# Grouped attention in a two-layer decoder: head turns moved between the two sides of the probability turns

## The chip, the cores and the metric

The kernel runs on one core of one Trainium2 chip. The metric is the device time of one execution in microseconds; the median of three runs before the change is 1094.67 us (1092.79 to 1095.51). The engines are TensorE (PE, with its weight load PEld), VectorE (DVE), ScalarE (ACT), GpSimd (POOL) and SyncE (SP), which issues most of the DMAs. Each engine works through its own list of instructions in order; semaphores tie the lists together.

## The reference

A decoder of two layers over four sequences of 256 tokens of width 256: a recurrent gate, experts chosen by token, a ternary projection, causal attention with 16 heads, grouped attention, a mixture of experts. The change touches only the grouped attention, which is, for 8 groups g of 2 query heads each and head width 128:

```python
q = _ln(_fp8_linear_pertensor(ln_out, wq, ...), qln_w, qln_b)    # (b, s, g, 2, 128)
k = _ln(_fp8_linear_pertensor(ln_out, wk, ...), kln_w, kln_b)    # (b, s, g, 128)
v = _fp8_linear_pertensor(ln_out, wv, ...)
core = _gqa(q, k, v)             # softmax(q k / sqrt(128)) v, per head
qx = _ln(_fp8_linear_pertensor(ln_out, wqx, ...), qxln_w, qxln_b)
kx, vx = split(einsum('bsi,oi->bso', ctx, w_kv_x)); kx = _ln(kx, kxln_w, kxln_b)
xout = _gqa(qx, kx, vx)
cat = concatenate([core, xout])
return einsum('bsi,oi->bso', _div_clamp_fp8(cat, proj_smooth), wproj) * (...)
```

"Side 0" is the attention over the tokens themselves (q, k, v), "side 1" the one over the context (qx, kx, vx). In each of them the head vectors are divided by their own root of the variance; the mean is taken out by centring the weights.

## The kernel before

The function front_stage holds everything but the mixture of experts. Its last part is a pipeline over 32 items, one for each group and sequence (four sequences of group 0, then four of group 1, and so on). A Slot n works on three items at once: it projects item n, scores item n-1, averages item n-2 and adds the output of item n-3. Slots 0 to 31 project, slots 1 to 32 score, slots 2 to 33 average, slots 3 to 34 output. There are 35 slots. In slots 0 to 27 the weights of the next group are also turned (transposed) and split into a high and a low half, two fills a slot: weights 0 and 1 in the first slot of a group, 2 and 3 in the second, 4 and 5 in the third, 6 and 7 in the fourth. I call these slots 0/1, 2/3, 4/5 and 6/7. Slot n with n mod 4 = 1 is a slot 2/3.

The order of each engine is written out by hand in its own function visit:

- PE (line 877): the first half of the projection (project_item(o, 0), L799 and L814), the two weight fills (next_weights, L765 and L767), the turns of the probabilities of item n-2 (turn_item_probs, L825: side 0 in two fills, then side 1 in two fills, four turns of 128x128 each), the second half of the projection, the turns of the heads of item n-1 (turn_item_heads, L838: three fills of four turns), in slot 1 alone two fills of tokens (L555), then average_item (L849), output_item (L873) and score_item (L861).
- ACT (line 1139): the high halves of the weights (L1066, L1074; weights 4 and 5 are only copied, L1070), the first copy of each side of the turned probabilities (take_item_probs, L1094), squares with their sums and the values from the projection's four fills (take_projection, L1086 and L1088), queries and keys from the head fills (take_item_heads, L1101, L1108, L1101), the averages (L1122), the exponentials of both sides (softmax_item, L1134).
- DVE (line 1496): the low halves of the weights (take_weight, L1437 and L1442; called w_lo in this text; none for weights 4 and 5), the second copy of each side of the probabilities (L1454), the rounding of the averages to fp8 (quantise_item, L1469, L196 to L199), the normalisation of the heads, read from all four projection fills (normalise_item, L1462), the addition of the output (add_item, L1494), the maxima of the scores (item_max, L1476), the division by the softmax sums, called the finish (finish_softmax, L1483 and L1486, once for each side). In slot 1 the fp8 rounding of the second half of the tokens (quantise, L1420 to L1425) follows the normalisation.
- POOL: one root per item (head_scale, L1662 and L1663), after the last squares, before the normalisation; and the split of the rounded tokens (L1669).

All results of PE go to PSUM, eight banks of 128x512 floats. The class Fills holds the plan: a fill has a bank and a number, and PE may start it (claim) when the fill before it in that bank has been drained by its reader. plan_slot (line 280) sets the order. The projection uses banks 0 to 3. All else turns round in banks 4 to 7, by the helper ring, which gives fill j of a slot bank 4 + j mod 4:

```python
WEIGHTS, PROBS_T, HEADS_T, OUT, ADD, SCORES = 0, 2, 6, 9, 11, 12
```

So the weights lie in banks 4 and 5, the probabilities of side 0 in 6 and 7, those of side 1 in 4 and 5, the heads in 6, 7 and 4, the averages in 5 and 6, the output in 7, the scores in 4 to 7. turn_item_heads also waits until the normalisation of the item before has drained the four projection fills; score_item waits until queries and keys are read; average_item waits until both copies of a side are made.

Of the kernel before, what the change touches and what calls it, by code (L numbers as in the profile page):

```python
# [28 lines left out]
ACT = mybir.ActivationFunctionType  # L29
# [250 lines left out]
def plan_slot(f, o):  # L280


    def ring(*fills_of):
        for j in fills_of:
            f.plan(4 + j % 4, ("slot", o.n, j))

    if o.projects:
        f.plan(0, ("proj", o.n, 0))
        f.plan(1, ("proj", o.n, 1))
    if o.n == 0:  # L290
        f.plan(4, ("Yc", 1, 0))
        f.plan(5, ("Yc", 1, 1))
    if o.weights:
        ring(WEIGHTS, WEIGHTS + 1)
    if o.averages:
        ring(*range(PROBS_T, HEADS_T))
    if o.projects:
        f.plan(2, ("proj", o.n, 2))
        f.plan(3, ("proj", o.n, 3))
    if o.scores:  # L300
        ring(*range(HEADS_T, OUT))
    if o.n == 1:
        f.plan(5, ("xT", "Q", 1, 0))
        f.plan(6, ("xT", "Q", 1, 1))
    if o.averages:
        ring(OUT, OUT + 1)
    if o.outputs:
        ring(ADD)
    if o.scores:
        ring(*range(SCORES, SCORES + 4))  # L310
# [93 lines left out]
def front_stage(nc, c, a):  # L404

    with Stage(nc) as st:
# [88 lines left out]
        with nc.Block() as block:  # L495
# [52 lines left out]
            def _(pe):  # L548
# [268 lines left out]

                def turn_item_probs(o):
                    for side in range(2):
                        pe.wait_ge(probs_ready, 2 * o.n + (side - 3))  # L820
                        for kt in range(2):
                            name = ("slot", o.n, PROBS_T + 2 * side + kt)
                            bank = fills.claim(pe, name)
                            for i in range(4):
                                last = pe.transpose(c.ps[:, bank, i * P:(i + 1) * P],  # L825
                                                    c.probs[:, side, i // 2, i % 2, kt * P:(kt + 1) * P], c.ident[:])
                            fills.filled(last, name)

# [48 lines left out]
                def visit(o):  # L877
# [6 lines left out]
                    if o.averages:  # L884
                        turn_item_probs(o)
                    if o.projects:
                        project_item(o, 1)
                    if o.scores:
                        turn_item_heads(o)
                    if o.n == 1:  # L890
# [60 lines left out]
            def _(act):  # L951
# [137 lines left out]

                def take_item_probs(o):  # L1090
                    for i in (0, 2):
                        name = ("slot", o.n, PROBS_T + i)
                        bank = fills.wait_full(act, name)
                        fills.drain(act.activation(c.probsT[:, i, :], c.ps[:, bank, :], ACT.Copy), name)  # L1094

# [43 lines left out]
                def visit(o):  # L1139
# [7 lines left out]
                    if o.averages:  # L1147
                        take_item_probs(o)
                    if o.projects:
                        take_projection(o, 0)  # L1150
                        take_projection(o, 1)
                    if o.scores:
                        take_item_heads(o)
                    if o.n == 1:
# [71 lines left out]
            def _(v):  # L1226
# [222 lines left out]

                def take_item_probs(o):  # L1450
                    for i in (1, 3):
                        name = ("slot", o.n, PROBS_T + i)
                        bank = fills.wait_full(v, name)
                        fills.drain(v.tensor_copy(c.probsT[:, i, :], c.ps[:, bank, :]), name)  # L1454

# [40 lines left out]
                def visit(o):  # L1496
                    if o.weights:
                        next_weights(o)
                    if o.averages:
                        take_item_probs(o)  # L1500
                    if o.outputs:
                        quantise_item(o)
                    if o.projects:
                        normalise_item(o)
# [533 lines left out]
```

## Time and profile before

| | before |
|---|---|
| median of three runs | 1094.67 us |
| the profiled execution's own time | 1086.79 us |
| its span, first to last instruction | 1085.2 us |
| PE busy | 968.6 us, 89% |
| DVE busy | 702.7 us, 65% |
| ACT busy | 596.6 us, 55% |
| POOL busy | 127.8 us, 12% |

Busy time counts what an engine executes, not what it waits for. PE's instructions overlap in its pipeline: the end of one lies behind the start of the next, so a row's length of n instructions is the sum of their intervals and a tail. The idle time in square brackets is that just before the row's first instruction, with the instruction whose semaphore ended it. The grouped part reaches from about 307 us (slot 0) to 960 us.

### The profile page before, as it was taken

How to read it: one execution, taken by the hardware profiler on the slowest of the kernel's cores; microseconds unless marked ns; L12 is line 12 of the kernel's file. 1: busy time of each engine (PE TensorE's matmuls, PEld its weight loads, DVE VectorE, ACT ScalarE, POOL GpSimd, SP SyncE). 2: the span in 40 equal slices, each digit the busy share in tenths (PEclk: the TensorE clock that was granted, in tenths of full speed). 3: DMA queues.
4: the chain of work that ended last, by engine and by line, in shares of the span. 5: the costliest groups of instructions: out<-in, count | busy, mean ns of one | idle time of the engine just before them, and what ended most of it. 6: DMA issues, size and time to landing. Idle time of an engine off the chain costs nothing. (4 is left out here: it accounts for less than half of the span.)

```text
span 1085.2 us, 16461 instructions
## 1 busy us (share of the span) xinstructions
PE 968.6 (89%) x5766; PEld 738.8 (68%) x5766; DVE 702.7 (65%) x1575; ACT 596.6 (55%) x2166; POOL 127.8 (12%) x126
## 2 busy tenths in 40 slices
PE   6989987998756899999999999999999999759597
PEld 3656655575545788878788888878888787544354
DVE  4655535577865676767676776767777676646554
ACT  4342324454625676767767676776767676413131
POOL 2000201000132211010101001010111101000000
PEclk9999997999887799999999999999999999869899
DMA  6010000000100010100100100100100300000000
GB/s 200 1 59 1 0 1 1 2 2 2 60 1 1 1 60 1 50 11 1 60 1 1 60 1 1 60 1 2 59 1 2 110 7 1 1 1 0 20 0 19
DMA packets 23122, 23.23 MB, mean 21 GB/s; under 512 B 3010, under 2 KB 22019, under 8 KB 23043
## 3 DMA queue, kind: packets, MB, share of 16 engines
q1 hardware_dynamic: 22944, 22.17, 6.5%
q8 instruction: 46, 0.75, 0.3%
q14 instruction: 34, 0.27, 0.1%
q10 hardware_dynamic: 98, 0.03, 0.0%
HBM read 21.15 MB, written 1.05 MB: 20 GB/s over the span
## 5 line engine op out<-in xcount | busy, mean ns | idle before, releaser
L1134 ACT ACTIVATE group_probs<-ps,score_bias 128x256 f32<-128x256 f32 x256 | 117.3, 484 | 112.5 <-DVE score_bias L1476 112.5
L799 PE MATMUL ps<-group_w_hi,xq 128*128 128x256 f32 (+1 forms) x512 | 133.4, 301 | 18.7 <-POOL xq L1669 11.2
L799 PE MATMUL ps<-group_w_lo,xq 128*128 128x256 f32 (+1 forms) x512 | 123.9, 284 | 0.0
L1462 DVE TENSOR_TENSOR group_heads<-ps,head_rstd 128x384 f32<-128x384 f32 x128 | 62.4, 550 | 87.0 <-POOL head_rstd L1663 87.0
L849 PE MATMUL ps<-group_probsT,group_values 128*128 128x512 f32 x256 | 116.7, 599 | 0.8 <-issue 0.8
L861 PE MATMUL ps<-group_kT,group_qT 128*128 128x256 f32 x512 | 115.9, 379 | 1.1 <-ACT group_qT L1101 1.1
L799 PEld LDWEIGHTS ps<-group_w_hi,xq 128*128 128x128 f32 x512 | 100.3, 196 | 21.2 <-DVE group_heads L1462 7.9
L1086 ACT ACTIVATE group_squares<-ps 128x128 f32<-128x128 f32 x384 | 106.5, 321 | 13.3 <-PE ps L799 11.9
L861 PEld LDWEIGHTS ps<-group_kT,group_qT 128*128 128x128 f32 x512 | 95.0, 190 | 13.5 <-issue 1.8
L1476 DVE TENSOR_REDUCE score_bias<-ps 128x2 f32<-128x512 f32 x128 | 88.2, 691 | 21.1 <-PE ps L861 21.1
L799 PEld LDWEIGHTS ps<-group_w_lo,xq 128*128 128x128 f32 x512 | 100.6, 196 | 0.7
L1086 ACT ACTIVATION_READ_ACCUMULATOR group_squares<-ps 128x1 f32 x384 | 93.3, 254 | 0.0
L825 PE MATMUL ps<-ident,group_probs 128*128 128x128 f32 x512 | 71.7, 281 | 18.2 <-DVE group_probs L1486 8.7
L873 PE MATMUL ps<-group_wp_hi,group_cat 128*128 128x256 f32 x256 | 76.4, 335 | 4.0 <-DVE group_cat L199 4.0
L849 PEld LDWEIGHTS ps<-group_probsT,group_values 128*128 128x128 f32 x256 | 46.8, 193 | 47.9 <-issue 47.9
L825 PEld LDWEIGHTS ps<-ident,group_probs 128*128 128x128 f32 x512 | 57.4, 143 | 29.3 <-DVE group_probs L1486 22.7
L1486 DVE TENSOR_SCALAR group_probs<-group_probs,score_inv 128x256 f32<-128x256 f32 x256 | 73.1, 349 | 2.3
L1663 POOL TENSOR_TENSOR head_rstd<-head_sum,minus_half 128x12 f32<-128x12 f32 x32 | 72.7, 2271 | 2.7
L1122 ACT ACTIVATE group_cat_y<-ps,vec_inv 128x256 bf16<-128x256 f32 x128 | 57.1, 528 | 24.9 <-PE ps L849 23.7
L814 PE MATMUL ps<-group_w_x,ctxT 128*128 128x256 f32 x256 | 67.3, 386 | 0.0
L1662 POOL TENSOR_SCALAR head_sum<-head_sum 128x12 f32<-128x12 f32 x32 | 6.5, 202 | 493.0 <-ACT group_values L1088 493.0
L873 PE MATMUL ps<-group_wp_lo,group_cat 128*128 128x256 f32 x256 | 63.9, 287 | 0.0
(265 smaller groups left out, 1928.8 us busy)
## 6 DMA issues: line engine op xcount, KB each, us to landing
group_raw_p<-in_L_xattn_wproj_dram SPq DMA_DIRECT2D x16, 256.0 KB, 3.8
group_raw_w<-in_L_xattn_wq_dram SPq DMA_DIRECT2D x8, 256.0 KB, 2.8
group_raw_w<-in_L_xattn_wqx_dram SPq DMA_DIRECT2D x8, 256.0 KB, 3.0
group_raw_w<-in_L_xattn_w_kv_x_dram SPq DMA_DIRECT2D x16, 128.0 KB, 3.4
x_all<-in_x_dram SPq DMA_DIRECT2D x2, 512.0 KB, 5.9
front_work<-in_ctx_dram SPq DMA_DIRECT2D x1, 1024.0 KB, 6.6
group_raw_w<-in_L_xattn_wk_dram SPq DMA_DIRECT2D x8, 128.0 KB, 3.0
group_raw_w<-in_L_xattn_wv_dram SPq DMA_DIRECT2D x8, 128.0 KB, 3.4
```

The source lines that it names most:

```text
L799: last = pe.matmul(c.ps[:, bank, at:at + width], x_, w[:, k, col:col + width], start=k == 0 and m == 0, stop=k == KD - 1 and m == 1)
L814: last = pe.matmul(c.ps[:, bank, 256:512], c.ctxT[:, b, k, t * P:(t + 1) * P], c.w_x[par][:, k, :], start=k == 0, stop=k == KD - 1)
L825: last = pe.transpose(c.ps[:, bank, i * P:(i + 1) * P], c.probs[:, side, i // 2, i % 2, kt * P:(kt + 1) * P], c.ident[:])
L849: last = pe.matmul(c.ps[:, bank, :], c.values[:, o.seq_of_average, kt, side, :], c.probsT[:, 2 * side + kt, :], start=kt == 0, stop=kt == 1)
L861: last = pe.matmul(c.ps[:, bank, t * S:(t + 1) * S], c.qT[:, side, h, t * P:(t + 1) * P], c.kT[:, side, :], start=True, stop=True)
L873: last = pe.matmul(c.ps[:, bank, t * D:(t + 1) * D], c.cat[:, i, t * P:(t + 1) * P], w[:, i, :], start=i == 0 and m == 0, stop=i == 3 and ...
L1086: act.activation(c.squares[:, t, 3 * i + h, :], c.ps[:, bank, h * HD:(h + 1) * HD], ACT.Square, accum_out=c.head_sum[:, t, 3 * i + h:3 * i ...
L1134: last = act.activation(c.probs[:, side, h, t, :], c.ps[:, fills.bank(name), t * S:(t + 1) * S], ACT.Exp, bias=c.score_bias[:, i:i + 1], a ...
L1462: fills.drain(v.tensor_tensor(c.heads[:, o.par, t, 3 * i:3 * i + 3, :], c.ps[:, fills.bank(name), 0:3 * HD].rearrange("p (h n) -> p h n", ...
L1476: v.tensor_reduce(c.score_bias[:, i:i + 2], c.ps[:, bank, :].rearrange("p (t n) -> p t n", n=S), AX.X, ALU.max, negate=True).then_inc(nega ...
L1486: ins = v.tensor_scalar(p, p, c.score_inv[:, 4 * side + i:4 * side + i + 1], None, ALU.mult)
L1663: pool.tensor_tensor(rstd, total, c.minus_half[:], ALU.pow).then_inc(rstd_ready, 1)
```

## The change

In plan_slot the probabilities of side 0 keep banks 6 and 7. The three head fills follow in banks 4, 5 and 6, then side 1 of the probabilities in banks 7 and 4, and only then the second half of the projection. PE, ACT and DVE follow in their lists: PE turns side 0, the heads, side 1, and then makes the second half of the projection; ACT copies side 0, reads the heads, copies side 1, and then does squares and values of both halves; DVE copies side 0, rounds the averages of the item before, copies side 1, and then normalises. What is computed and the number of instructions stay the same.

```diff
@@ plan_slot
     if o.averages:
-        ring(*range(PROBS_T, HEADS_T))
+        f.plan(6, ("slot", o.n, PROBS_T))
+        f.plan(7, ("slot", o.n, PROBS_T + 1))
+    if o.scores:
+        f.plan(4, ("slot", o.n, HEADS_T))
+        f.plan(5, ("slot", o.n, HEADS_T + 1))
+        f.plan(6, ("slot", o.n, HEADS_T + 2))
+    if o.averages:
+        f.plan(7, ("slot", o.n, PROBS_T + 2))
+        f.plan(4, ("slot", o.n, PROBS_T + 3))
     if o.projects:
         f.plan(2, ("proj", o.n, 2))
         f.plan(3, ("proj", o.n, 3))
-    if o.scores:
-        ring(*range(HEADS_T, OUT))
@@ PE, visit
                     if o.averages:
-                        turn_item_probs(o)
+                        turn_item_probs(o, 0)
+                    if o.scores:
+                        turn_item_heads(o)
+                    if o.averages:
+                        turn_item_probs(o, 1)
                     if o.projects:
                         project_item(o, 1)
-                    if o.scores:
-                        turn_item_heads(o)
@@ ACT, visit
                     if o.averages:
-                        take_item_probs(o)
+                        take_item_probs(o, 0)
+                    if o.scores:
+                        take_item_heads(o)
+                    if o.averages:
+                        take_item_probs(o, 1)
                     if o.projects:
                         take_projection(o, 0)
                         take_projection(o, 1)
-                    if o.scores:
-                        take_item_heads(o)
@@ DVE, visit
                     if o.averages:
-                        take_item_probs(o)
+                        take_item_probs(o, 0)
                     if o.outputs:
                         quantise_item(o)
+                    if o.averages:
+                        take_item_probs(o, 1)
                     if o.projects:
                         normalise_item(o)
```

turn_item_probs and the two take_item_probs get the side as an argument instead of a loop over both.

## Rows read from the trace of the kernel before

**Rows 1.** The page: PE and the others; granted TensorE clock in 40 slices of 27 us.

```profile
PE 968.6 (89%) x5766; PEld 738.8 (68%) x5766; DVE 702.7 (65%) x1575; ACT 596.6 (55%) x2166; POOL 127.8 (12%) x126
...
PEclk9999997999887799999999999999999999869899
```

**Rows 2.** Groups by line, 380 to 840 us: count | busy us, mean ns | idle before, releasers.

```profile
L825 PE MATMUL ps<-ident,group_probs 128*128 128x128 f32 x397 | 54.9, 277 | 9.5 <-DVE group_w_lo L1437 5.7 <-DVE group_wp_lo L1442 3.8
```

**Rows 3.** Timeline of PE in a slot 2/3 and after: start, length, instruction [idle].

```profile
569.56 1.04 PE L825 MATMUL ps<-ident,group_probs 128*128 128x128 f32 x8
571.20 1.08 PE L825 MATMUL ps<-ident,group_probs 128*128 128x128 f32 x8 [0.61 <-DVE group_w_lo L1437]
...
581.49 3.62 PE L861 MATMUL ps<-group_kT,group_qT 128*128 128x256 f32 x16
...
588.30 2.13 PE L825 MATMUL ps<-ident,group_probs 128*128 128x128 f32 x16
```

**Rows 4.** Timeline of DVE in the same slot: last finish, w_lo, end of the rounding.

```profile
569.40 1.14 DVE L1486 TENSOR_SCALAR group_probs<-group_probs,score_inv 128x256 f32<-128x256 f32 x4
570.45 1.12 DVE L1437 SCALAR_TENSOR_TENSOR group_w_lo<-ps,w_scale,group_w_hi 128x128 fp32r<-128x128 f32 x4
...
575.04 1.23 DVE L199 TENSOR_TENSOR group_cat<-group_cat_y,group_cat_e 128x1024 fp32r<-128x1024 bf16 x1
```

**Rows 5.** Timeline of ACT and DVE from 571.20 to the first exponential.

```profile
571.87 0.60 ACT L1094 ACTIVATE group_probsT<-ps 128x512 f32<-128x512 f32 x1 [0.69 <-PE ps L825]
572.36 0.27 ACT L1086 ACTIVATE group_squares<-ps 128x128 f32<-128x128 f32 x1
...
575.99 0.92 ACT L1101 ACTIVATE group_qT<-ps,query_affine 128x512 f32<-128x512 f32 x1
576.65 1.17 ACT L1108 ACTIVATE group_kT<-ps,vec 128x256 f32<-128x256 f32 x2
577.55 0.94 ACT L1101 ACTIVATE group_qT<-ps,query_affine 128x512 f32<-128x512 f32 x1
...
578.91 1.95 DVE L1462 TENSOR_TENSOR group_heads<-ps,head_rstd 128x384 f32<-128x384 f32 x4 [2.65 <-POOL head_rstd L1663]
...
581.68 0.69 DVE L1494 TENSOR_TENSOR x_all<-x_all,ps 128x512 f32<-128x512 f32 x1 [0.82 <-PE ps L873]
582.55 0.69 DVE L1476 TENSOR_REDUCE score_bias<-ps 128x2 f32<-128x512 f32 x1 [0.18 <-PE ps L861]
...
584.14 0.47 ACT L1134 ACTIVATE group_probs<-ps,score_bias 128x256 f32<-128x256 f32 x1 [3.52 <-DVE score_bias L1476]
```

**Rows 6.** Timeline of PE: side 1 in slot 28, the first without weights.

```profile
853.73 1.09 PE L825 MATMUL ps<-ident,group_probs 128*128 128x128 f32 x8 [0.66 <-DVE group_probs L1486]
```

**Rows 7.** Timeline: exponentials of slot 4/5; side 1, w_lo and exponentials of 6/7 and 0/1.

```profile
602.29 0.47 ACT L1134 ACTIVATE group_probs<-ps,score_bias 128x256 f32<-128x256 f32 x1 [3.52 <-DVE score_bias L1476]
...
608.24 1.22 PE L825 MATMUL ps<-ident,group_probs 128*128 128x128 f32 x8 [0.54 <-DVE group_wp_lo L1442]
...
621.32 0.47 ACT L1134 ACTIVATE group_probs<-ps,score_bias 128x256 f32<-128x256 f32 x1 [3.52 <-DVE score_bias L1476]
...
626.79 1.77 DVE L1437 SCALAR_TENSOR_TENSOR group_w_lo<-ps,w_scale,group_w_hi 128x256 fp32r<-128x256 f32 x4 [0.32 <-ACT group_w_hi L1066]
...
627.81 0.63 PE L825 MATMUL ps<-ident,group_probs 128*128 128x128 f32 x4 [0.16 <-DVE group_w_lo L1437]
...
641.13 0.47 ACT L1134 ACTIVATE group_probs<-ps,score_bias 128x256 f32<-128x256 f32 x1 [3.53 <-DVE score_bias L1476]
```

**Rows 8.** Timeline of DVE and ACT in slots 1 and 2.

```profile
333.62 1.13 DVE L1437 SCALAR_TENSOR_TENSOR group_w_lo<-ps,w_scale,group_w_hi 128x128 fp32r<-128x128 f32 x4 [5.70 <-ACT group_w_hi L1066]
...
342.92 0.43 DVE L1420 TENSOR_SCALAR front_work<-front_work 128x1024 bf16<-128x1024 bf16 x1 [0.42 <-ACT front_work L1057]
...
365.27 0.27 ACT L1086 ACTIVATE group_squares<-ps 128x128 f32<-128x128 f32 x1
...
375.10 0.47 ACT L1134 ACTIVATE group_probs<-ps,score_bias 128x256 f32<-128x256 f32 x1 [1.61 <-DVE score_bias L1476]
```

More of the change, by code:

```diff
@@ L816, in project_item, with turn_item_probs @@
                     fills.filled(last, name)
[L818 to L827, printed above, removed]
+                def turn_item_probs(o, side):
+                    pe.wait_ge(probs_ready, 2 * o.n + (side - 3))
+                    for kt in range(2):
+                        name = ("slot", o.n, PROBS_T + 2 * side + kt)
+                        bank = fills.claim(pe, name)
+                        for i in range(4):
+                            last = pe.transpose(c.ps[:, bank, i * P:(i + 1) * P],
+                                                c.probs[:, side, i // 2, i % 2, kt * P:(kt + 1) * P], c.ident[:])
+                        fills.filled(last, name)
                 def turn_item_heads(o):
@@ L1088, in take_projection, with take_item_probs @@
                         act.activation(c.values[:, o.s, t, i, :], c.ps[:, bank, 3 * HD:4 * HD], ACT.Copy).then_inc(proj_read, 1)
[L1090 to L1094, printed above, removed]
+                def take_item_probs(o, side):
+                    name = ("slot", o.n, PROBS_T + 2 * side)
+                    bank = fills.wait_full(act, name)
+                    fills.drain(act.activation(c.probsT[:, 2 * side, :], c.ps[:, bank, :], ACT.Copy), name)
                 def take_item_heads(o):
@@ L1448, in next_weights, with take_item_probs @@
                         take_weight(("slot", o.n, WEIGHTS + i), 2 * o.s + i, o.g + 1)
[L1450 to L1454, printed above, removed]
+                def take_item_probs(o, side):
+                    name = ("slot", o.n, PROBS_T + 2 * side + 1)
+                    bank = fills.wait_full(v, name)
+                    fills.drain(v.tensor_copy(c.probsT[:, 2 * side + 1, :], c.ps[:, bank, :]), name)
                 def normalise_item(o):
```

## The prediction

> **What bounds the kernel now.** I read the page first: TensorE (PE) is busy for 89% of the span, the other engines far less [rows 1], so time is won or lost only where PE pauses, or through a loop that sets the length of a slot. The groups of instructions come next. In the even part of the grouped stage, 380 to 840 us, the probability turns (L825) carry PE's pauses, 9.5 us, and all of them are put down to DVE's low halves of the weights [rows 2]. Then I read the timeline of single slots, because they repeat to 0.02 us. In the slot that turns weights 2 and 3, side 0 of the probabilities starts at 569.56 and side 1 at 571.20. Both sides without a pause are 16 turns in 2.13, tail included, so I count 0.9 for the eight turns of one; side 1 pauses for the rest, 0.61 by the row, and its releaser is DVE's w_lo [rows 3]: side 1 fills banks 4 and 5, which the weights held. That DVE instruction stands right behind the finish of the softmax [rows 4]. I call side 1's start, the point that waits for the weights' banks, the **gate**.
>
> What feeds the gate is a loop through all engines, as these rows show [rows 5]: gate 571.20; ACT's first copy 571.87; squares 572.36; the heads' three reads 575.99, 576.65, 577.55; DVE's normalisation 578.91, released by Pool (POOL); DVE's add 581.68 after 0.82 us idle; first maximum 582.55; first exponential 584.14. From there to the next gate come eight exponentials, two finishes and w_lo; 569.40 and 570.45 are the last two of these one slot earlier [rows 4]. So the path runs gate, PE (turns, projection, average, output), scores, maxima, exponentials, finish, w_lo, gate. ACT's squares, POOL and the normalisation lie beside it, with 0.82 us to spare at the add and 0.18 at the maximum [rows 5].
>
> **The change part by part.** On PE nothing is added or removed: the 12 head turns only stand before side 1 instead of behind the projection's second half. PE's work between the gate and the scores, 571.20 to 581.49 [rows 3], is the same to 0.1 us.
>
> *The wait for bank 4 is not removed.* Side 1 now fills banks 7 and 4, but the first head fill takes bank 4 directly after the weights, and it comes at the same place in PE's order, 0.9 after side 0. The gate moves from side 1 to the heads; it still waits for w_lo. Only the four slots without weights (28 to 31) lose a wait there, since heads need no probability; it is 0.66 us each [rows 6].
>
> *ACT.* The heads' reads (0.66, 0.90, and 0.66 for the third by the first) move ahead of the squares: 2.22 us. ACT goes through squares and values in 3.63 (572.36 to 575.99) and is their limit; PE's second projection half moves back by 12 turns, some 1.3, ACT by 2.2, so ACT stays it. After the change, counted from the gate: first read at 0.67 (571.20 to 571.87), three reads to 2.89, the copy of side 1 (0.49, from 571.87 to 572.36) to 3.38, squares, then 6.55 from squares to normalisation (572.36 to 578.91): 9.93 instead of 7.71 [rows 5].
>
> *DVE.* Its order is weights, copy, quantise, copy, normalise. The second copy now stands behind the quantisation, which ends 5.07 after the gate today [rows 4] and would end, with the copy, at about the same time; the average needs it later than that. Free. But normalise, add, maxima are in line behind POOL's answer: 9.93 + 1.87 (four normalisations in 1.95, less the 0.08 by which neighbours overlap) + 0.61 (add, 0.69 less 0.08) + 0.61 + 0.69 (two maxima) + 0.02 = 13.73 from gate to first exponential. Today it is 12.94 [rows 5]. The spare time of the add is used up and 0.79 is left over. **The side chain becomes the path.** Queued behind the late normalisation on DVE are the maxima, behind them ACT's exponentials, then DVE's finish and w_lo, and PE waits for that at the gate.
>
> *The other slots of a group* [rows 7]. Weights 4 and 5: today 602.29 less 588.30 less 0.9 = 13.09 from where the heads will start; lag 0.64. Weights 6 and 7: 608.24 to 621.32, 13.08; lag 0.65. Weights 0 and 1: 627.81 to 641.13, 13.32; here the second head fill waits 0.14 longer for bank 5, so 13.87 and a lag of 0.55. The gates pass the lag on, except: slot 4/5 has no DVE weights, so its gate is PE's own and only its exponentials are 0.64 late; slot 0/1 has 0.32 of idle DVE time before w_lo, which absorbs that much. Take G as the delay at the gate of slot 2/3 (its own 0.79 ends in the free gate of 4/5): exponentials of 4/5 at G + 0.64, gate of 6/7 the same, its exponentials G + 1.29, gate of 0/1 at G + 0.97, its exponentials and with them the next gate of 2/3 at G + 1.52: **1.52 per group of four slots**.
>
> *The start* (slots 1 and 2, before the last half of the tokens is quantised) [rows 8]. In slot 1 the heads come ahead of the projection and meet w_lo, which runs 333.62 to 334.75: bank 4 is free after half, 334.18, and PE follows 0.18 later as it does at 571.20 (570.45 + 0.56 [rows 4]): gate 334.36. Normalisation at 334.36 + 9.93 - 0.49 (no copy) = 343.80, done 345.67; the quantisation of the other half is queued behind it on DVE and started at 342.92: **+2.75**. PE and POOL wait for it through the whole conversion. In slot 2 ACT's squares (365.27) fall behind by up to 2.22, less what ACT waited for anyway; I take 1.9, as DVE went from normalisation to maxima without idling and the exponentials (375.10) move alike: **+1.9**.
>
> *The sum.* 4.65 at the first exponentials of slot 2; slot 3 (weights 6/7) +0.65, slot 4 -0.32 +0.55: 5.53 at the gate of slot 5. Five groups of 1.52 to slot 25: 13.13. Slots 26 and 27: +0.64 +0.65 = 14.42. Slots 28 to 31: the 0.66 pause at side 1 goes [rows 6], but side 0 must now wait for a finish that is late by the same lag, so nothing is gained or lost. Last two items: side 1's copy behind the quantisation can hold the average for a moment, 0.1. **Together +14.5 us.** The profiled execution takes 1086.79 (span 1085.2); the median of the runs is 1094.67, 7.9 above it. I add the sum to the median: **1109.2**.
>
> *Bounds.* If the spare time hid the lag, only the start would be left, +4.65; nothing below follows from that mechanism. If nothing absorbed anything, each of 27 gates would be 0.79 late: 21.3 + 4.65 = 26. The sizes come from repeating rows, so I am nearer to the middle; 0.2 of lag either way changes the sum by 4.
>
> **The rivals.**
>
> *Faster: the pauses go.* If heads filled the hole before side 1 and the lag stayed under the 0.82 of spare time, the pauses of L825 would vanish: 9.5 us and four times 0.66 [rows 2, 6], -12.1 us: 1082.6. For it: heads depend on no softmax, and ACT idles 3.52 us before each slot's exponentials [rows 5]. Against it: the releaser is w_lo, not the probabilities, in the timeline of every slot with DVE weights, and bank 4 is claimed at the same place. It decides at a bank 4 that is drained by the end of side 0, some 570.45; w_lo only starts then [rows 3, 4]. The Trainium skill, "Perfetto Trace Analysis", Matmuls, says that independent matmul groups should rotate through different PSUM banks so that reading one overlaps filling the next; by that rule alone the new plan, with side 1 off the weights' banks, should help, and would give this rival's time. The trace shows the same neighbour left on bank 4. Chance 0.08.
>
> *The change hardly does anything* (0.07): the gate only changes its name, the spare time at add and maxima covers the lag, and the 2.64 us of slots 28 to 31 pay for part of the start. +4.65 - 2.64 = +2.0: 1096.7. It needs ACT to get through heads and squares 0.8 us faster than it does today [rows 5].
>
> *Part of the lag is hidden* (0.10): half of what follows the start, 4.65 + 4.9 = 9.6: 1104.3, inside my range.
>
> *Slower than forecast: TensorE's clock falls.* The granted clock is at its upper level, 2.4 GHz, from the fifteenth slice to the end of the stage [rows 1], with pauses of 0.2 to 0.7; it is lower in the two slices before, where PE waited on the conversion of the tokens. The pauses I forecast grow to some 1.4 us in two of four slots. If a tenth of the stage's 576 us of work ran at 1.2 GHz, it would take twice as long: +29 on top of the +14.5, 1138. Against it: nothing as short as this lowered it in this stage. The Trainium skill, "TensorE: Matmul & The Clock Gate", Part 1, says that the array is throttled by default and activity releases it. No run here yet shows what these pauses do. Chance 0.05.
>
> **How the numbers follow.** Forecast 0.70 (1109.2, from 1102 to 1117 by 0.3 of lag, three times in each of six groups, and 2 us at the start); half hidden 0.10; hardly anything 0.07; faster 0.08; clock 0.05. The range 1098 to 1118 leaves out the faster, the neutral and the clock case, 0.20. A difference under 0.3% (3.3 us) can't be told from no change by a measurement of this kernel. Faster by more 0.08, within 0.07, slower 0.85.
>
> **What would show it.** The pause at the heads' turns (L838 today), not at side 1, released by w_lo, of some 1.2 to 1.4 us in slots 2/3 and 6/7; side 1 with hardly a pause; DVE's add no longer idle before it (0.82 today) and the maxima back to back with it; POOL's answer some 2.2 us later after the gate; ACT's idle time before the exponentials down by some 2 us; groups that are 1.5 us longer than today's. I am wrong if the normalisation still starts within 8.5 us of the gate, or if the gate waits no longer than today. The least certain steps are ACT's pace with heads first, and the start.

## The result, and the profile after

The changed kernel takes 1101.44 us (median of six runs, 1100.65 to 1105.85); the kernel before takes 1092.97 in the six runs beside them (1090.72 to 1095.51). The ratio is 1.0089, 95% interval 1.0063 to 1.0114; a second measurement of the same two kernels, further down, gives 1.0100 (1.0065 to 1.0135). So it is slower, by 9.7 to 10.9 us by the two ratios. The forecast was +14.5 us and 1109.2: the sign and the mechanism are as foretold, the size is too large.

The page of the profiled execution after (1100.65 us, span 1099.0): busy time, and the granted clock in 40 slices.

```profile
span 1099.0 us, 16461 instructions
...
PE 971.5 (88%) x5766; PEld 742.4 (68%) x5766; DVE 684.9 (62%) x1575; ACT 592.9 (54%) x2166; POOL 127.6 (12%) x126
...
PEclk9999997998868899999999999999999999869889
```

PE does the same 5766 matmuls in 3 us more of busy time and 13.8 us more of span. In the clock row, as in that of [rows 1], the upper level is unbroken between the low slices ahead of the even part and those behind it.

The same page's costliest groups (line, engine, operation, out<-in, shapes, count | busy us, mean ns of one | idle before them, and its releaser):

```profile
L1140 ACT ACTIVATE group_probs<-ps,score_bias 128x256 f32<-128x256 f32 x256 | 117.1, 483 | 132.3 <-DVE score_bias L1483 132.3
L1469 DVE TENSOR_TENSOR group_heads<-ps,head_rstd 128x384 f32<-128x384 f32 x128 | 62.5, 550 | 157.4 <-POOL head_rstd L1672 157.4
...
L1483 DVE TENSOR_REDUCE score_bias<-ps 128x2 f32<-128x512 f32 x128 | 79.8, 683 | 0.7 <-PE ps L866 0.7
```

The same two DVE lines on the page of before:

```profile
L1462 DVE TENSOR_TENSOR group_heads<-ps,head_rstd 128x384 f32<-128x384 f32 x128 | 62.4, 550 | 87.0 <-POOL head_rstd L1663 87.0
...
L1476 DVE TENSOR_REDUCE score_bias<-ps 128x2 f32<-128x512 f32 x128 | 88.2, 691 | 21.1 <-PE ps L861 21.1
```

DVE's normalisation waits 157.4 us for POOL's root in all (87.0 before), and the maxima behind it hardly wait any more (0.7, 21.1 before): where these lines stand one behind the other without idling, the side chain is the path.

The groups of PE by line in the even part, 384 to 853 us, beside [rows 2] (L830 turns the probabilities, as L825 did; L843 the heads, as L838 did):

```profile
L830 PE MATMUL ps<-ident,group_probs 128*128 128x128 f32 x400 | 52.3, 274 | 1.4 <-DVE group_probs L1493 0.7
...
L843 PE MATMUL ps<-ident,group_heads 128*128 128x128 f32 x300 | 39.9, 277 | 17.5 <-DVE group_w_lo L1445 9.4 <-DVE group_wp_lo L1450 7.7
```

The 9.5 us pause at the probabilities is gone from there. It stands at the heads with 17.5 us, behind the same releaser, the low halves of the weights.

The timeline of one slot 2/3 (start, length, engine, line, operation; in brackets the idle time before it and its releaser), to be laid beside [rows 3 to 5]:

```profile
577.99 1.04 PE L830 MATMUL ps<-ident,group_probs 128*128 128x128 f32 x8
...
579.45 1.12 DVE L1445 SCALAR_TENSOR_TENSOR group_w_lo<-ps,w_scale,group_w_hi 128x128 fp32r<-128x128 f32 x4
...
580.20 1.52 PE L843 MATMUL ps<-ident,group_heads 128*128 128x128 f32 x12 [1.17 <-DVE group_w_lo L1445]
...
580.87 0.78 ACT L1107 ACTIVATE group_qT<-ps,query_affine 128x512 f32<-128x512 f32 x1 [1.20 <-PE ps L843]
...
581.54 1.01 ACT L1114 ACTIVATE group_kT<-ps,vec 128x256 f32<-128x256 f32 x2
581.55 1.04 PE L830 MATMUL ps<-ident,group_probs 128*128 128x128 f32 x8
...
583.10 0.61 ACT L1100 ACTIVATE group_probsT<-ps 128x512 f32<-128x512 f32 x1
...
583.58 0.30 ACT L1093 ACTIVATE group_squares<-ps 128x128 f32<-128x128 f32 x1
...
584.33 0.68 DVE L1461 COPY group_probsT<-ps 128x512 f32<-128x512 f32 x1
...
585.14 3.60 PE L854 MATMUL ps<-group_probsT,group_values 128*128 128x512 f32 x8
...
590.14 1.95 DVE L1469 TENSOR_TENSOR group_heads<-ps,head_rstd 128x384 f32<-128x384 f32 x4 [5.13 <-POOL head_rstd L1672]
...
592.01 0.68 DVE L1501 TENSOR_TENSOR x_all<-x_all,ps 128x512 f32<-128x512 f32 x1
...
592.60 2.48 DVE L1483 TENSOR_REDUCE score_bias<-ps 128x2 f32<-128x512 f32 x4
...
593.92 0.48 ACT L1140 ACTIVATE group_probs<-ps,score_bias 128x256 f32<-128x256 f32 x1 [4.31 <-DVE score_bias L1483]
```

The gate is now the heads' start, 580.20, and still w_lo's: the first half of L1445 ends 0.56 after 579.45, PE follows 0.19 later. ACT's first square is 3.38 behind the gate (1.16 before), the normalisation 9.94 behind it (7.71 before), the first exponential 13.72 (12.94 before). DVE's add has no idle time before it, and the four maxima have become one row without gaps.

**Where the 13.8 us of the two spans lie (13.9 before rounding).** I divided both traces at the start of slot 1 and measured from there; the second pair is a second profiled execution of each kernel (e5 and e6 below). All in us:

| | before | after | difference | second pair |
|---|---|---|---|---|
| slot 1 starts | 326.57 | 328.21 | +1.64 | +1.78 |
| from there: first exponentials of slot 2 | 48.53 | 52.62 | +4.09 | +5.45 |
| of slot 27 | 521.96 | 534.46 | +12.50 | +13.79 |
| of slot 31 | 594.57 | 606.45 | +11.88 | +13.17 |
| the experts' turns start | 641.29 | 654.01 | +12.72 | +11.57 |
| from there to the end | 117.3 | 116.8 | -0.49 | -0.77 |

The group of four slots is 75.74 long before (75.73 in the second profile) and 77.03 after (77.00 to 77.03 in the second): +1.29. Within each profile the groups between slots 4 and 27 repeat to 0.04 or better.

### The profile page after: what moved, and what is told of

Read it like the earlier page. It is cut to its first block and busy times, and to the rows that moved or that the text cites. A ratio compares the mean times of both kernels' runs of the same rounds, so it can differ in the third digit from the quotient of the medians.

```text
span 1099.0 us, 16461 instructions
## 1 busy us (share of the span) xinstructions
PE 971.5 (88%) x5766; PEld 742.4 (68%) x5766; DVE 684.9 (62%) x1575; ACT 592.9 (54%) x2166; POOL 127.6 (12%) x126
## 5 line engine op out<-in xcount | busy, mean ns | idle before, releaser
L1469 DVE TENSOR_TENSOR group_heads<-ps,head_rstd 128x384 f32<-128x384 f32 x128 | 62.5, 550 | 157.4 <-POOL head_rstd L1672 157.4
L1093 ACT ACTIVATE group_squares<-ps 128x128 f32<-128x128 f32 x384 | 110.2, 353 | 14.0 <-PE ps L805 12.1
L1093 ACT ACTIVATION_READ_ACCUMULATOR group_squares<-ps 128x1 f32 x384 | 100.3, 287 | 0.0
L854 PEld LDWEIGHTS ps<-group_probsT,group_values 128*128 128x128 f32 x256 | 49.0, 192 | 47.9 <-issue 46.4
L1483 DVE TENSOR_REDUCE score_bias<-ps 128x2 f32<-128x512 f32 x128 | 79.8, 683 | 0.7 <-PE ps L866 0.7
L830 PE MATMUL ps<-ident,group_probs 128*128 128x128 f32 x512 | 70.3, 282 | 9.5 <-DVE group_probs L1493 7.0
L830 PEld LDWEIGHTS ps<-ident,group_probs 128*128 128x128 f32 x512 | 59.3, 145 | 15.0 <-DVE group_probs L1493 11.3
L843 PE MATMUL ps<-ident,group_heads 128*128 128x128 f32 x384 | 51.6, 281 | 18.7 <-DVE group_w_lo L1445 10.6
```

The costliest lines, as they stand in the source:

```text
L830: last = pe.transpose(c.ps[:, bank, i * P:(i + 1) * P], c.probs[:, side, i // 2, i % 2, kt * P:(kt + 1) * P], c.ident[:])
L854: last = pe.matmul(c.ps[:, bank, :], c.values[:, o.seq_of_average, kt, side, :], c.probsT[:, 2 * side + kt, :], start=kt == 0, stop=kt == 1)
L1093: act.activation(c.squares[:, t, 3 * i + h, :], c.ps[:, bank, h * HD:(h + 1) * HD], ACT.Square, accum_out=c.head_sum[:, t, 3 * i + h:3 * i ...
L1469: fills.drain(v.tensor_tensor(c.heads[:, o.par, t, 3 * i:3 * i + 3, :], c.ps[:, fills.bank(name), 0:3 * HD].rearrange("p (h n) -> p h n", ...
L1483: v.tensor_reduce(c.score_bias[:, i:i + 2], c.ps[:, bank, :].rearrange("p (t n) -> p t n", n=S), AX.X, ALU.max, negate=True).then_inc(nega ...
```

## The experiments

My theory: heads ahead of side 1 put 2.22 us of ACT's reads ahead of the squares; the chain squares, root, normalisation, add, maxima is then longer than PE's own way to the scores, and each slot is late by what is left over; w_lo at the gate passes it on. Rival A: the pause at bank 4 is itself the cause, since the gate was moved but not removed. Rival B: the projection's second half, now behind all turns, or DVE's copy behind the quantisation, is late. Lengths of groups are given from the trace; ratios are against the kernel before on the same chip.

**Both kernels again (e5, e6).** No edit.

> The kernel before, unchanged, profiled once more. Between the two profiled executions the span grew by 13.8 us, between the medians by 8.5 (ratio 1.0089, 1.0063 to 1.0114). Theory (the profiled execution of before happened to have little time at TensorE's lower clock level ahead of the grouped stage): groups of 75.74 us again, the same 644 us from slot 1's start to the mixture of experts within 2 us, and a span 4 to 8 us longer than 1085.2, all of it ahead of slot 1 or where the clock is low. Rival (the steady slots themselves differ between executions): groups that differ by some tenths of a us.

> The changed kernel, unchanged, profiled once more beside the kernel before: groups of 77.03 again, 12 to 13 us more than before from slot 1's start to the mixture of experts; the times at 8 to 11 us above those of before.

Before: 1093.87, 1.001 (0.9987 to 1.0034). After: 1102.32, 1.0100 (1.0065 to 1.0135). Groups 75.73 and 77.00 to 77.03. The table above has both pairs. Between the two executions of one kernel the start of slot 1 moves by 2.1 to 2.2 us and the last 117 us by 0.5 to 0.8; the groups don't move.

**The weights out of the turns' way, in the changed kernel (e1).** Banks 2 and 3 are idle between the normalisation and the projection's second half.

```diff
     if o.weights:
-        ring(WEIGHTS, WEIGHTS + 1)
+        f.plan(2, ("slot", o.n, WEIGHTS))
+        f.plan(3, ("slot", o.n, WEIGHTS + 1))
```

> The changed kernel with the two weight fills of a slot planned into banks 2 and 3, where the second half of the projection comes later; banks 4 to 7 are then free of weights. Theory (a gate at the weights' bank, fed by a side chain of ACT, POOL and DVE that is 0.8 us late): the heads no longer pause (1.17, 1.05 and 0.39 us in the slots 2/3, 6/7 and 0/1 of the changed kernel), though the first exponential still comes 13.7 us after the heads' start; PE alone sets the slots, and a group of four takes about 74.0 us instead of 77.0. That is 19 us less than the changed kernel and some 6 us less than the kernel before. Rival (the late side chain is the loss by itself, whatever bank the heads use): groups stay near 77 us and the pause only moves to side 1 of the probabilities.

1103.11, 1.0089 (1.0062 to 1.0117), with groups of 75.96 instead of 77.03. Two things happened. In slot 0 the projection's second half, which fills the same banks 2 and 3, now waited for w_lo, and slot 1 began some 12 us later: a loss of the edit, not of the question. In the even part the pause went from the heads to side 1. Its row by line, 384 to 845 us, and the timeline of a slot 2/3:

```profile
L831 PE MATMUL ps<-ident,group_probs 128*128 128x128 f32 x384 | 50.3, 274 | 13.8 <-DVE group_probsT L1462 12.9 <-DVE group_probs L1494 1.0
...
L844 PE MATMUL ps<-ident,group_heads 128*128 128x128 f32 x288 | 36.7, 274 | 0.1
```

```profile
588.34 1.47 PE L844 MATMUL ps<-ident,group_heads 128*128 128x128 f32 x12
...
588.65 1.12 DVE L1446 SCALAR_TENSOR_TENSOR group_w_lo<-ps,w_scale,group_w_hi 128x128 fp32r<-128x128 f32 x4
...
589.69 0.68 DVE L1462 COPY group_probsT<-ps 128x512 f32<-128x512 f32 x1
...
590.52 1.07 PE L831 MATMUL ps<-ident,group_probs 128*128 128x128 f32 x8 [0.71 <-DVE group_probsT L1462]
```

Side 1 starts in bank 7, which DVE's copy of side 0 drains, and that copy stands behind w_lo on DVE. So w_lo held PE through a second door: its place in DVE's queue, not only its bank, holds PE. The group is 1.07 shorter, where my theory had 3 and the rival recorded above nothing. That rival was right that the pause only moves to side 1; neither had the size.

**The same in the kernel before (e2).** The same edit.

> The kernel before with the same one edit, weights in banks 2 and 3. Theory: the pauses at side 1 (0.61, 0.54, 0.34) go, since in the slot without DVE weights side 1 does not wait for the finish either; groups of 74.0 instead of 75.7, 11 us less than before. The four slots 28 to 31 keep their pause of 0.66. Rival (the pauses at side 1 are the softmax's, not the bank's): they stay, released by the finish, and the time is within 2 us of before.

1087.06, 0.9939 (0.9917 to 0.9962): 7.5 us less where I expected 11, with the same loss in slot 0. Groups 73.47, 2.26 shorter than before, and no pause at any turn between 384 and 840 us. Side 0 and side 1 fill 6, 7 and 4, 5 here, so PE's turns start in no bank whose reader is queued behind w_lo.

**Slot 1 alone in the old order (e3).** The changed kernel, with heads behind the projection in slot 1 on PE and ACT:

```diff
-                    if o.scores:
+                    if o.scores and o.n > 1:
...
+                    if o.n == 1:
+                        turn_item_heads(o)
```

> The changed kernel, but in slot 1 alone the heads are turned and read in the old place, after the projection. Theory: the rounding of the second half of the tokens starts as early after slot 1's start as before, 16.4 us instead of 18.5; 2.1 us less than the changed kernel, all before the steady slots, groups unchanged at 77.0. Rival (the start costs nothing, the conversion of the tokens waits for something else): no change.

1101.3, 1.0074 (1.0052 to 1.0097). From slot 1's start the quantisation began at 16.12 us (18.49 and 18.68 in the changed kernel, 16.35 and 15.74 in the one before), the first exponentials of slot 2 at 49.91 (52.62 and 52.88; before 48.53 and 47.43). The groups stayed at 77.02. So the changed order costs the start 2.4 to 2.6 us in slot 1 against this run, and 2.1 to 2.9 against the kernel before; the rest of the start's loss belongs to slot 2. The runs' median hardly shows it (0.1 to 1.0 us less than the changed kernel's): that is less than executions of one kernel differ by. In the profiled one slot 1 starts only at 333.59 us, with 52.8 us at the lower clock level ahead of it (46.3 and 45.9 in the two profiles of the changed kernel). The granted clock between 74 and 84 us was 0.77 in it, in the first profile of the changed kernel 1.00.

**ACT's delay alone, in the old order (e4).** Four extra reads of PSUM into scratch ahead of the squares, 2.0 us, all else as before:

```diff
+                def idle_reads(o):
+                    bank = fills.bank(("slot", o.n, PROBS_T + 2))
+                    for i in range(4):
+                        last = act.activation(c.scratch[:, i, :], c.ps[:, bank, :], ACT.Copy)
```

> The kernel before with four more reads of the last probability fill on ACT (to a scratch tile that nobody reads), some 2.0 us put ahead of the squares, in the place where the change puts the heads' reads. Orders and banks stay those of before. Theory (the side chain is 0.8 to 1.0 us from being the path): the normalisation comes 2.0 us later after the gate, DVE's 0.82 us of idle time before the add goes, the exponentials start about 0.5 us later after the gate, and a group is 0.6 to 0.9 us longer: 5 to 7 us in all. Rival (the heads' new place on bank 4 is the loss and the side chain has room): within 1 us of before.

1123.5, 1.0283 (1.0256 to 1.031): five times what I expected. Groups 79.86, +4.1. The timeline of a slot 2/3 tells why, and it isn't my mechanism:

```profile
591.24 0.95 ACT L1110 ACTIVATE group_qT<-ps,query_affine 128x512 f32<-128x512 f32 x1
...
592.24 1.98 PE L849 MATMUL ps<-group_probsT,group_values 128*128 128x512 f32 x4 [0.89 <-ACT group_qT L1110]
```

In the old order the heads' reads come last on ACT, and the average fills bank 6 behind the first head fill. Whatever is put ahead of the squares makes those reads late as well, and PE's average waits, in every slot. The changed order reads the heads ahead of the squares, so that a delay behind those reads can't hit them. As a test of the theory it was badly made, because the edit delayed two consumers at once.

**POOL's root twice, in the old order (e7).** A delay of 2.27 us that touches the side chain and nothing else:

```diff
+                    pool.tensor_tensor(c.pool_scratch[:], total, c.minus_half[:], ALU.pow)
                     pool.tensor_tensor(rstd, total, c.minus_half[:], ALU.pow).then_inc(rstd_ready, 1)
```

> The kernel before with POOL's root taken twice for each item, the first time into a scratch tile: 2.27 us more in the side chain between ACT's squares and DVE's normalisation, about the 2.22 us by which the change delays it. Orders, banks, ACT and PE stay those of before (the extra ACT work of the last try also held up ACT's own reads, which POOL's does not). Theory (the late side chain is what makes the change slow): nearly the whole loss appears without the change: the normalisation 10.0 us after side 1's start, DVE's idle time before the add gone, the exponentials 0.8 us later after side 1's start, groups of 77.0 to 77.3 instead of 75.7, +11 to +13 us in all with the start. Rival (the heads' wait on the weights' bank in its new place is the loss): DVE's 0.82 us of idle time hides it, within 3 us of before.

1116.59, 1.0226 (1.0191 to 1.026). The timeline of a slot 2/3:

```profile
586.77 1.08 PE L825 MATMUL ps<-ident,group_probs 128*128 128x128 f32 x8 [1.22 <-DVE group_w_lo L1437]
...
592.15 2.27 POOL L1663 TENSOR_TENSOR pool_scratch<-head_sum,minus_half 128x12 f32<-128x12 f32 x1
...
594.39 2.27 POOL L1664 TENSOR_TENSOR head_rstd<-head_sum,minus_half 128x12 f32<-128x12 f32 x1
...
596.69 1.95 DVE L1462 TENSOR_TENSOR group_heads<-ps,head_rstd 128x384 f32<-128x384 f32 x4 [4.87 <-POOL head_rstd L1664]
...
598.56 0.68 DVE L1494 TENSOR_TENSOR x_all<-x_all,ps 128x512 f32<-128x512 f32 x1
...
600.46 0.47 ACT L1134 ACTIVATE group_probs<-ps,score_bias 128x256 f32<-128x256 f32 x1 [4.30 <-DVE score_bias L1476]
```

Normalisation 9.92 and first exponential 13.69 behind side 1's start, pause at the gate 1.22, no idle time before the add: the picture of the changed kernel (9.94, 13.72, 1.17), made in the old order by the side chain's delay alone. The group is 77.94, though, 0.9 longer than the changed kernel's. The surplus is the old order's own: side 1 also waits for its probabilities, 0.73 in slot 4/5, and slots 28 to 31 take 18.9 each instead of 18.15. With heads between the sides, side 1 waits 0.11 at most in those slots, and they take 18.00. In all this run is 24 us slower than the kernel before, where I expected 11 to 13: six groups at 2.2, 3 us in slots 28 to 31, and the rest at the start, where slot 1 begins 4 to 6 us later and slot 2's exponentials come another 3 to 4 us later.

**The root left out, in both orders (e8, e9).** POOL writes ones instead of the root, so queries and keys aren't normalised; the side chain is 2.1 us shorter.

```diff
-                    pool.tensor_tensor(rstd, total, c.minus_half[:], ALU.pow).then_inc(rstd_ready, 1)
+                    pool.tensor_scalar(rstd, total, 0.0, 1.0, ALU.mult, ALU.add).then_inc(rstd_ready, 1)
```

> The changed kernel with POOL's root left out (the scale of the heads is set to one by a short instruction, so the heads are not normalised): 2.0 us less in the side chain, orders and banks those of the change. Theory: the normalisation comes 7.9 us after the heads' start, DVE waits for the output before the add again, groups fall from 77.0 to 75.7 as before the change, though the heads still wait on the weights' bank; 10 to 12 us less than the changed kernel. Rival (the bank in its new place is the loss): groups stay at 77.0 and the time within 2 us of the changed kernel.

> The kernel before with POOL's root left out in the same way as in the last try (the heads are not normalised). Theory: in the old order the side chain has room, so nothing changes in the steady slots: groups of 75.74, within 1.5 us of before. What is then left between this kernel and the changed kernel without the root (groups of 75.49, slots 28 to 31 of 17.47 instead of 18.15) is the gain of the heads' new place alone, some 4 us. Rival (the root is on the path before the change too): groups shorter than 75.5.

Changed order: 1088.16, 0.9952 (0.993 to 0.9973), 13 us less than the changed kernel's median. Old order: 1092.88, 0.999 (0.9968 to 1.0013), no difference. Groups 75.48 and 75.70. The changed order without the root, in a slot 2/3, and its row of L843 in 384 to 853 us:

```profile
576.53 1.52 PE L843 MATMUL ps<-ident,group_heads 128*128 128x128 f32 x12 [0.60 <-DVE group_w_lo L1445]
...
584.41 1.95 DVE L1469 TENSOR_TENSOR group_heads<-ps,head_rstd 128x384 f32<-128x384 f32 x4 [3.06 <-POOL head_rstd L1672]
...
587.01 0.69 DVE L1501 TENSOR_TENSOR x_all<-x_all,ps 128x512 f32<-128x512 f32 x1 [0.65 <-PE ps L878]
...
589.46 0.47 ACT L1140 ACTIVATE group_probs<-ps,score_bias 128x256 f32<-128x256 f32 x1 [3.52 <-DVE score_bias L1483]
```

```profile
L843 PE MATMUL ps<-ident,group_heads 128*128 128x128 f32 x300 | 39.9, 277 | 9.4 <-DVE group_w_lo L1445 5.7 <-DVE group_wp_lo L1450 3.8
```

The normalisation is 7.88 behind the gate, the add idles 0.65 again, the first exponential is at 12.93, and the pause at the heads is 0.60 and 9.4 us in sum, as side 1's was before [rows 2, 3]. **This settles the cause.** The pause at bank 4 alone costs the changed order nothing more than it cost the old one; the 8 us by which the pauses grew, and the slower groups, come from the side chain. The old order has room in that chain and takes no notice of 2.1 us less. It also gives the price of the heads' new place by itself: 0.22 per group and 0.68 in each of slots 28 to 31, some 4 us to the good. So rival A falls. Rival B falls with it: this run has the projection's second half and DVE's copy in their new places, and its groups are shorter than the old ones. The averages, which stand behind both, also start as early after the gate as before: 4.94 us, by 585.14 - 580.20 in the changed kernel and by this row of the kernel before, whose gate is at 571.20:

```profile
576.14 3.60 PE L849 MATMUL ps<-group_probsT,group_values 128*128 128x512 f32 x8
```

DVE's copy (584.33 and 0.68) ends just 0.13 ahead of them.

**The weights in banks 2 and 3 from slot 2 on (e10, e11).** Slots 0 and 1 keep their plan, so that the start isn't touched. e10 is the kernel before with this; e11 the changed kernel, where DVE also copies side 0 ahead of w_lo, against e1's second door.

```diff
-    if o.weights:
+    if o.weights and o.n < 2:
         ring(WEIGHTS, WEIGHTS + 1)
+    elif o.weights:
+        f.plan(2, ("slot", o.n, WEIGHTS))
+        f.plan(3, ("slot", o.n, WEIGHTS + 1))
```

> The kernel before with the weight fills in banks 2 and 3 from slot 2 on; slots 0 and 1 keep banks 4 and 5, because in slot 0 the second half of the projection waited 9.1 us for the weights' low halves. Theory: groups of 73.5 us as in the first try of this, no loss at the start: 14 us less than before, about 1079, ratio 0.987. Rival (the wait in slot 0 only showed time that is lost there anyway): the start is not recovered and the time is that of the first try, 0.994.

> The changed kernel with the weight fills in banks 2 and 3 from slot 2 on, and with DVE's copy of side 0 ahead of the low halves of the weights; both waits that the changed order had (heads on the weights' bank, side 1 in bank 7 behind DVE's copy) are then gone or under 0.2 us. Theory: groups of 73.6 to 74.2 us instead of 77.0, 18 to 20 us less than the changed kernel, but 3 to 5 us more than the old order with the same banks, for the start. Rival (DVE's queue is still late, as when side 1 waited for its copy): pauses of 0.4 to 0.7 at side 1 and groups of 75 to 76.

e10: 1075.77, **0.984 (0.9816 to 0.9864)**, groups 73.50. e11: 1082.83, 0.9909 (0.9885 to 0.9933), groups 73.69, start 5 us later as in the changed kernel. Both beat both kernels, and e10 is the best. Of the 17 us between the medians of e10 and the kernel before, the traces place 14 between the start of slot 1 and slot 27 (506.82 us against 520.84 in e5). A slot 2/3 of e10:

```profile
566.55 2.12 PE L828 MATMUL ps<-ident,group_probs 128*128 128x128 f32 x16
...
567.44 1.12 DVE L1440 SCALAR_TENSOR_TENSOR group_w_lo<-ps,w_scale,group_w_hi 128x128 fp32r<-128x128 f32 x4
...
568.43 0.36 PE L802 MATMUL ps<-group_w_hi,xq 128*128 128x256 f32 x1
```

Both sides are one row of 16 turns without a gap, while DVE reads the weights beside them; the projection's second half needs bank 2 only at 568.43, after the first half of w_lo has drained it (567.44 and 0.56).

The new order of heads and sides gains nothing on top of it: e11's groups are 0.19 longer than e10's, and its start later.

## Why the prediction was right, and where its sizes were off

- **The wait for bank 4 is not removed.** Right. It is at the heads, released by w_lo, 1.17 in the slot shown and 1.04 in slot 6/7 (1.2 to 1.4 forecast), and e8 shows it at 0.60 once the side chain is short.
- **ACT.** Right to 0.01: squares at gate + 3.38, normalisation at + 9.94 against 9.93.
- **DVE: the second copy is free.** Right: the averages start no later (4.94 behind the gate in both kernels, though the copy ends only 0.13 ahead of them), and DVE idles 5.13 before the normalisation. Normalise, add and maxima in line: 13.72 against 13.73. e7 and e8 show both directions of it.
- **ACT's idle time before the exponentials.** The step in "What would show it" is wrong in sign. I had it down by 2 us because the reads go ahead; it rose from 3.52 to 4.31, by the lag of 0.79. The reads moved from one side of the squares to the other, so ACT is done as early as before after the gate and only waits longer for the maximum.
- **The group of four.** 1.29 against 1.52. Slot 2/3 to 6/7 +0.62 (0.64 forecast), 6/7 to 0/1 +0.22 (0.33), 0/1 to 2/3 +0.45 (0.55). The mis-sized terms are the two around slot 0/1: I took its second head fill as 0.14 late at bank 5, but the 12 head turns run through (lag 0.45, not 0.55), and I took its spare 0.32 as all of the cover, where 0.42 is covered. From slot 2 to slot 27 the trace gives 8.4 us where my terms make 9.8.
- **The start.** Slot 1 +2.1 and +2.9 (2.75 forecast), to slot 2's exponentials +4.1 and +5.45 (4.65): right, in the middle of what two profiles give. The kernel before takes 1.1 us less for that stretch in its second profile, with 18.6 us of it at the lower clock level where the first has 23.6.
- **Slots 28 to 31.** "Nothing gained or lost" missed 0.6 us: they take 18.00 each instead of 18.15. The wait is where the prediction put it, at side 0, for the late finish; side 1 waits for DVE's copy, 0.11. Slot 29 of the changed kernel:

```profile
884.04 1.09 PE L830 MATMUL ps<-ident,group_probs 128*128 128x128 f32 x8 [0.21 <-DVE group_probs L1493]
...
886.55 1.06 PE L830 MATMUL ps<-ident,group_probs 128*128 128x128 f32 x8
```

Its size was off (0.35 in slot 28, then 0.21 to 0.22, in place of 0.66 at side 1). The loop now runs from the first exponential over the first finish to side 0 (3.38), to the heads (0.93) and through the late side chain to the next exponential (13.69): 18.00. Before, it ran over the second finish to side 1 (5.20) and from there 12.95: 18.15. With the late side chain in the old order (e7) the same way takes 18.92.

- **The faster rival** held a part of the truth: a bank that is free makes the pauses go, as e10 shows, and the heads' new place is worth 4 us where the side chain has room. It falls because this plan put heads on bank 4 and because the side chain was asked for 2.22 and had less to give. What it had is more than the 0.82 against which the rival's "for" was set: from the normalisation to the first exponential it went from 5.23 to 3.78 us, so 1.45 was given, by the idle time at the add (0.82) and at the first two maxima (0.18 and 0.17) and, for the rest, by instructions that now overlap. The sum of 13.73 had counted all of that. The Trainium skill, "Perfetto Trace Analysis", Matmuls, wants independent matmul groups to rotate through different banks, so that reading one overlaps the next. The runs agree with it where the next user of the bank comes late enough (e10, 0.984). They show in e1 (0.35 to 1.09 us at side 1) what it leaves out: a bank without weights holds PE as well, if its own reader is queued behind a late instruction.
- **The clock rival** fell: between 368 and 937 us of the changed kernel the granted clock is 1.00, its upper level of 2.4 GHz, with pauses up to 1.2 us in it. The rival's price was also mis-stated: a tenth of 576 us of work that takes twice as long adds 58 us, not 29. No run shows such a fall here. The row of the windows view (stretch, its length, busy time and instructions of PE, PEld, DVE, ACT, POOL, the granted clock, DMA share, GB/s):

```profile
368.00:937.00 569.00, 546.82 (x3420) 458.65 (x3417) 375.82 (x828) 399.17 (x1689) 74.01 (x60) 1.00 0.07 23
```

**The total.** I forecast 1109.2 and 1101.44 was measured, 7.8 less. Of this, 1.7 is the base: the median of three that I added to was 1094.67, that of the six runs beside the changed kernel 1092.97. The other 6.0 lie between +14.5 and +8.5. From slot 1 to the experts I had 14.4 and 0.1; the two pairs of profiles give 12.7 and 11.6. That is 1.4 for six groups at 0.23, 0.6 for the last slots, and what then differs, 0.2 us one way and 0.9 the other, is no more than what executions of one kernel differ by.

The profiles themselves are 13.9 and 12.6 us apart in span, the medians 8.5 and, of the second measurement, 9.6. The time of each kernel comes in levels: the kernel before at about 1086.7, 1090.4, 1092.7 and 1095.2, the changed one at 1100.4 to 1101.6, once at 1103.0, and at 1105.5. The mean granted clock goes with them only roughly: 0.951 at both of the lower levels of the kernel before and 0.948 at the highest, 0.950 to 0.948 and 0.947 to 0.945 in the changed one. The first profiled execution of the kernel before was at its lowest level, 7.9 under the median to which I added the sum. Why the levels of the two kernels aren't the same distance apart, and which stretch the executions without a profile lose, is open: only a profile shows it. The sizes of the pipeline hold to 2 or 3 us; how near the difference of the medians comes to them depends, by a few us, on the levels that the runs fell into, and that part was not foreseen.

## What to carry to other kernels

A pause that names a reader is moved, not removed, when the next fill of the same bank takes the pausing one's place: ask for every bank who fills it next, who drains it, and what stands ahead of that reader on its engine. Before work is moved ahead of a chain that lies beside the path, read that chain's slack at every instruction where it meets the path on the way to the result (here 0.82 us at DVE's add and less at the maxima, 1.45 in all down to the first exponential): what exceeds it, 0.79 of 2.22 here, comes back at every point where the loop has no idle time of its own. And moving the fill that holds the bank into a bank that nobody needs for the moment cost four lines and gave 1.6%, where moving the heads ahead of side 1 lost 0.9%.

## What the runs showed of the hardware that I had not expected

A kernel that doesn't change moves by up to 9 us, and part of this can be laid to the granted clock. The kernel before ran at four levels from 1086.7 to 1095.2 us. Its low-clock stretches ahead of slot 1 make 41.2 us in one profile and 46.3 in the other (6.8 and 10.2 in the one at 302 us), and slot 1 starts 2.1 us later in the second. The mean granted clock of both is 0.951 all the same, with spans 3.7 us apart: it counts where a low stretch falls. From the first exponential of slot 31 to that of slot 32 the first takes 15.4 us, the second, with 3.4 us at the lower level from 927.5 us on, 17.1.

Pauses of 1.2 us, in two slots of every group, never lowered the clock within 569 us; but between 74 and 84 us of e3 and e6 it was 0.77 and 0.83, with PE busy for 9.75 and 10.00 of the 10, where both first profiles have 1.00 in the same stretch.

A delay of 2.3 us on a chain with 1.45 to spare cost 2.2 us per group of four slots when it was on POOL (e7), but one of 2.0 on ACT cost 4.1 (e4): what else was queued behind the delayed instruction counted for more than its length.
